# Attention: the turned FFN weight tile is split on POOL, and the inverse square roots of the q and k norms are one power operation each

## The reference

```python
q = (layernorm(x) @ Wq).reshape(B, Sq, H, D)
k = (ctx @ Wk).reshape(B, Skv, H, D)
v = (ctx @ Wv).reshape(B, Skv, H, D)
q = rmsnorm(q, gq)          # x * rsqrt(mean(x**2) + 1e-5) * g, over the 128 of a head
k = rmsnorm(k, gk)
attn = softmax(einsum('bqhd,bkhd->bhqk', q, k) * D ** -0.5)
x = x + einsum('bhqk,bkhd->bqhd', attn, v).reshape(B, Sq, H * D) @ Wo
```

## Time and profile before

| what | value |
|---|---|
| median of 3 runs | 2759.77 us (2758.46 to 2761.99) |
| profiled execution: its own time | 2749.03 us |
| its span | 2747.2 us |
| busy in the span | PE 2310.0 (84%), DVE 1898.2 (69%), POOL 1361.7 (50%), ACT 1235.3 (45%) |
| mean granted TensorE clock, of full speed | 0.911 |

### The profile page before, as it was taken

The page is one execution under the profiler, slowest core; times in us unless marked ns, Lnnn a source line. Parts: engine busy times, 40 slices in busy tenths (PEclk is TensorE's granted clock), DMA queues, the critical chain, the costliest instruction groups (busy, mean ns, idle before and its releaser), DMA issues. The chain is left out here.

```text
span 2747.2 us, 37910 instructions
## 1 busy us (share of the span) xinstructions
PE 2310.0 (84%) x10784; PEld 1774.8 (65%) x10785; DVE 1898.2 (69%) x3625; ACT 1235.3 (45%) x2129; POOL 1361.7 (50%) x1722
## 2 busy tenths in 40 slices
PE   3699999999999999998784898998998839459980
PEld 2687888878787878887533665665665426447770
DVE  6576777767677767776675989999999876412223
ACT  2353444544444444454483655655655412024440
POOL 0233333333243333332384888878988803478324
PEclk7799999999999999999886999999999958679995
DMA  7512232122322232220457555464665220565317
GB/s 276 206 62 101 85 109 86 62 90 85 109 85 76 76 109 85 85 77 28 142 202 237 176 180 184 173 197 151 205 195 158 86 89 16 201 201 175 130 54 256
DMA packets 136939, 363.84 MB, mean 132 GB/s; under 512 B 21280, under 2 KB 58912, under 8 KB 118560
## 3 DMA queue, kind: packets, MB, share of 16 engines
q1 hardware_dynamic: 123648, 328.36, 35.5%
q0 software_dynamic: 6320, 20.71, 2.4%
q10 hardware_dynamic: 6768, 12.32, 1.2%
HBM read 290.06 MB, written 71.30 MB: 132 GB/s over the span
## 5 line engine op out<-in xcount | busy, mean ns | idle before, releaser
L662 POOL TENSOR_SCALAR att_probs<-att_probs,att_recip 128x512 f32<-128x512 f32 x256 | 183.9, 722 | 402.5 <-DVE att_recip L743 398.1
L1837 POOL TENSOR_TENSOR mix_drive<-mix_du,mix_rows 128x512 f32<-128x512 f32 x256 | 326.5, 1282 | 61.4 <-DMA mix_rows<-bc_d 29.1
L585 ACT ACTIVATE att_probs<-att_s,att_bias,att_rq 128x512 f32<-128x512 f32 x256 | 199.9, 781 | 301.3 <-DVE att_bias L739 299.1
L1890 DVE TENSOR_TENSOR_SCAN mix_state<-mix_state,mix_drive 128x512 f32<-128x512 f32 x256 | 312.6, 1221 | 14.7 <-POOL mix_drive L1837 10.7
L1721 ACT ACTIVATE mix_state<-mix_delta,mix_a 128x512 f32<-128x512 f32 x256 | 176.7, 691 | 277.4 <-DVE mix_drive L1901 238.6
L1822 POOL TENSOR_TENSOR mix_y<-mix_y,mix_drive 128x512 f32<-128x512 f32 x180 | 230.6, 1281 | 79.0 <-DVE mix_drive L1901 79.0
L1630 PE MATMUL mix_down<-mix_wd,mix_hT 128*128 128x512 f32 x512 | 232.1, 596 | 8.7 <-DVE residual_x L1921 8.7
L738 DVE TENSOR_REDUCE att_nmax<-att_s 128x1 f32<-128x512 f32 x256 | 174.9, 683 | 64.7 <-PE att_s L101 64.7
L591 ACT CAST att_pT<-att_pt 128x512 fp32r<-128x512 f32 x256 | 143.4, 588 | 141.7 <-PE att_pt L442 137.6
L789 DVE TENSOR_TENSOR att_pT<-att_pt,att_pT 128x512 fp32r<-128x512 f32 x256 | 169.4, 682 | 44.6 <-ACT att_pT L591 44.2
L99 PE MATMUL att_w<-att_w_qkv,att_cx 128*128 128x256 f32 x512 | 161.9, 316 | 34.7 <-DVE att_w_qkv L725 26.7
(11 more groups left out here) (359 smaller groups left out, 6789.5 us busy)
## 6 DMA issues: line engine op xcount, KB each, us to landing
att_xn<-normT SPq DMA_DIRECT2D x32, 2048.0 KB, 9.2
mix_gu<-guT SPq DMA_DIRECT2D x64, 1024.0 KB, 8.3
mix_rows<-bc_d SPq DMA_DIRECT2D x128, 256.0 KB, 5.0
guT<-att_ffnT SPq DMA_DIRECT2D x32, 512.0 KB, 3.4
mix_wd<-wdT SPq DMA_DIRECT2D x16, 1024.0 KB, 7.8
slots<-exp_y ACTq DMA_DIRECT2D x47, 256.0 KB, 2.0
normT<-nrm_outT SPq DMA_DIRECT2D x4, 2048.0 KB, 9.1
exp_raw<-in_L_ffn_Wg SPq DMA_DIRECT2D x16, 512.0 KB, 5.8
```

Of the source, the lines that this page charges most:

```text
L585: act.activation(probs[:, n, :], ps_s[n % 2][:, :], ACT.Exp, bias=bias[:, n:n + 1], scale=rq[:, n:n + 1], accum_out=sums[:, n:n + 1]).then ...
L662: pool.tensor_scalar(probs[:, n, :], probs[:, n, :], recip[:, n:n + 1], 1.0, ALU.mult, ALU.mult).then_inc(s_pn, 1)
L1837: pool.tensor_tensor(drive[q % RING][:, :], du[i % DUS][:, :], rows[g % ROWS][:, 0, :], ALU.mult).then_inc(s_drive, 1)
L1890: dve.tensor_tensor_scan(h[:, :], h[:, :], drive[q % RING][:, :], 0.0, ALU.mult, ALU.add).then_inc(s_scan, 1)
```

## The change

Three things are changed, all in `stage_attention`.

1. The inverse roots. The three Newton steps on POOL and the two guess operations on DVE become one POOL operation, value to the power of a constant tile of -0.5, for k and for q.
2. The FFN tile. ACT, which wrote the hi of the turned tile to `fT`, now copies the whole float32 tile from PSUM back over `fraw` (`ffn_out`). POOL then makes both parts from it in SBUF (`split_ffn`), between `norm_p` 7 and the power of q. DVE's `ffn_lo` goes.
3. The waits. The FFN tile has semaphores of its own, so `turn_p(1, 1)`, which uses its PSUM bank, waits for ACT's copy and not for DVE. SP issues the load of `xn` as soon as the queries of j are done, ahead of its wait for the FFN tile; the load of the next FFN tile now waits for POOL's split, since `fraw` is used until then. At b = 0 the loads of weights stand ahead of that of `xn`.

```diff
@@ SP
+                sp.wait_ge(s_q, 2)
+                sp.dma_start(xn[:, :, :, :].bitcast(F32), xT[1]).then_inc(s_xn, 16)
                 def iteration(hp, b, last):
                     i = hp * B + b
-                    if not last:
-                        sp.wait_ge(s_q, 2 * i + 2)
-                        sp.dma_start(xn[:, :, :, :].bitcast(F32), xT[(b + 1) % B]).then_inc(s_xn, 16)
                     if b == 0 and not (isinstance(hp, int) and hp == PAIRS - 1):
...
+                    if not (isinstance(hp, int) and b >= B - 2):
+                        sp.wait_ge(s_q, 2 * i + 4)
+                        sp.dma_start(xn[:, :, :, :].bitcast(F32), xT[(b + 2) % B]).then_inc(s_xn, 16)
+                    sp.wait_ge(s_flo, i + 1)
                     if not last:
-                        sp.wait_ge(s_pt, TURNS * i + TB + 1)
                         load_ffn(hp + (b + 1) // B, (b + 1) % B)
-                    sp.wait_ge(s_ptlo, TURNS * i + TB + 1 + 2)
                     store_ffn(hp, b)
@@ PE, turn_p
-                    pe.wait_ge(s_ptlo, TURNS * i + n + 1)
+                    if h and k == 1:
+                        pe.wait_ge(s_fout, i + 1)
+                    elif h and k == 0:
+                        pe.wait_ge(s_ptlo, 8 * i + TB + 2)
+                    else:
+                        pe.wait_ge(s_ptlo, 8 * i + TB * h + k + 1)
@@ ACT
-                def ffn_hi(hp, i, b):
-                    act.wait_ge(s_pt, TURNS * i + TB + 1)
-                    act.wait_ge(s_fst, 16 * (i + 1))
-                    act.copy(fT[:, 0, :, :], ps_pt[(b + TB) % 2][:, :, :]).then_inc(s_fhi, 1)
+                def ffn_out(i, b):
+                    act.wait_ge(s_ft, i + 1)
+                    act.copy(fraw[:, :], ps_pt[(b + TB) % 2][:, :, :].rearrange("p k n -> p (k n)")).then_inc(s_fout, 1)
@@ POOL
-                def newton(own, out, value, guess, work):
...
+                def norm_k(j):
                     wait_apart(pool, s_kss, j + 1, s_pace)
-                    newton(own, rk[:, :], kss[:, :], kguess[:, :], work[:, :])
-                    pool.sem_inc(s_rk, 1)
+                    pool.tensor_tensor(rk[:, :], kss[:, :], power[:, :], ALU.pow).then_inc(s_rk, 1)
...
+                def split_ffn(i):
+                    parts = [fT[:, n, :, :].rearrange("p k n -> p (k n)") for n in range(2)]
+                    wait_apart(pool, s_fout, i + 1, s_pace)
+                    wait_apart(pool, s_fst, 16 * (i + 1), s_pace)
+                    pool.tensor_scalar(parts[0], fraw[:, :], 1.0, 1.0, ALU.mult, ALU.mult).then_inc(s_fhi, 1)
+                    wait_apart(pool, s_fhi, i + 1, s_pace)
+                    pool.tensor_tensor(parts[1], fraw[:, :], parts[0].bitcast(F32), ALU.subtract).then_inc(s_flo, 1)
...
                     if not last:
-                        norm_k(own, j)
+                        norm_k(j)
                     norm_p(i, 6)
                     norm_p(i, 7)
+                    split_ffn(i)
                     if not last:
-                        norm_q(own, j)
@@ DVE
-                    own.after(dve.tensor_scalar(kss[:, :], kss[:, :], 1.0 / D, RMS_EPS, ALU.mult, ALU.add))
-                    guess(own, kguess[:, :], kss[:, :]).then_inc(s_kss, 1)
+                    dve.tensor_scalar(kss[:, :], kss[:, :], 1.0 / D, RMS_EPS, ALU.mult, ALU.add).then_inc(s_kss, 1)
...
-                    ffn_lo(i, b)
                     o_lo(i, 0)
```

More of the change, by code:

```diff
@@ L260, in stage_attention @@
     RMS_EPS = 1e-5
-    NEWTON = 3
     scale = D ** -0.5
@@ L295, in stage_attention @@
         rq = m.sb("rq", [P, TB * HP])
-        kguess = m.sb("kguess", [P, TB * HP])
-        qguess = m.sb("qguess", [P, TB * HP])
-        work = m.sb("work", [P, TB * HP])
+        power = m.sb("power", [P, TB * HP])
         nmax = m.sb("nmax", [P, TB * HP])
@@ L331, in stage_attention @@
         s_pace = m.sem("pace")
-        s_fraw, s_fhi, s_fst = m.sem("ffn_raw_in"), m.sem("ffn_hi"), m.sem("ffn_stored")
+        s_fraw, s_ft, s_fout = m.sem("ffn_raw_in"), m.sem("ffn_turned"), m.sem("ffn_turned_out")
+        s_fhi, s_flo, s_fst = m.sem("ffn_hi"), m.sem("ffn_lo"), m.sem("ffn_stored")
         def pairs(eng, iteration):
@@ L636, in iteration @@
                         q_parts(j, 1)
-                    ffn_hi(hp, i, b)
+                    ffn_out(i, b)
                     o_hi(i, 0)
@@ L663, in norm_p @@
                                        ALU.mult).then_inc(s_pn, 1)
-                def newton(own, out, value, guess, work):
-                    cur = guess
-                    for _ in range(NEWTON):
-                        own.mark(pool.tensor_tensor(work, cur, cur, ALU.mult))
-                        own.wait_apart(s_pace)
-                        own.mark(pool.tensor_tensor(work, work, value, ALU.mult))
-                        own.wait_apart(s_pace)
-                        own.mark(pool.tensor_scalar(work, work, -0.5, 1.5, ALU.mult, ALU.add))
-                        own.wait_apart(s_pace)
-                        own.mark(pool.tensor_tensor(out, cur, work, ALU.mult))
-                        own.wait_apart(s_pace)
-                        cur = out
@@ L689, in _ @@
-                own = Steps(pool, s_pool)
-                square_k(0)
-                norm_k(own, 0)
-                norm_q(own, 0)
-                base = own.n
-                per_pair = B * base
-                def iteration(own, hp, b, last):
+                    pool.tensor_tensor(rq[:, :], qss[:, :], power[:, :], ALU.pow).then_inc(s_rq, 1)
+                def split_ffn(i):
[5 more added lines that the diff above has]
+                    pool.tensor_tensor(parts[1], fraw[:, :], parts[0].bitcast(F32), ALU.subtract).then_inc(s_flo, 1)
@@ L697, in iteration @@
+                pool.memset(power[:, :], -0.5).then_inc(s_power, 1)
+                square_k(0)
+                pool.wait_ge(s_power, 1)
+                norm_k(0)
+                norm_q(0)
+                def iteration(hp, b, last):
                     i = hp * B + b
@@ L705, in iteration @@
                     if not last:
-                        norm_k(own, j)
+                        norm_k(j)
                     norm_p(i, 6)
                     norm_p(i, 7)
+                    split_ffn(i)
                     if not last:
-                        norm_q(own, j)
-                with pool.Fori(0, PAIRS - 1) as hp:
-                    own = Steps(pool, s_pool, hp * per_pair + base)
-                    for b in range(B):
-                        iteration(own, hp, b, False)
-                own = Steps(pool, s_pool, (PAIRS - 1) * per_pair + base)
-                for b in range(B):
-                    iteration(own, PAIRS - 1, b, b == B - 1)
+                        norm_q(j)
+                pairs(pool, iteration)
             @block.vector
@@ L743, in row_recip @@
                     dve.reciprocal(recip[:, n:n + 1], sums[:, n:n + 1]).then_inc(s_rec, 1)
-                def guess(own, out, value):
-                    I32 = mybir.dt.int32
-                    own.after(dve.tensor_scalar(out.bitcast(I32), value.bitcast(I32), 1, None, ALU.logical_shift_right))
-                    return dve.tensor_scalar(out.bitcast(I32), out.bitcast(I32), -1.0, float(0x5F3759DF), ALU.mult, ALU.add)
                 def sum_k(own, j):
@@ L824, in _ @@
                 kt_lo(0, 1)
-                sum_q(own, 0)
+                sum_q(0)
                 v_lo(0, 0)
@@ L832, in _ @@
                 base = own.n
-                per_pair = B * (8 + 3 + 1) + 3
+                per_pair = B * (8 + 1) + 3
                 def iteration(own, hp, b, last):
@@ L873, in iteration @@
                     if not last:
-                        sum_q(own, j)
+                        sum_q(j)
                     pt_lo(i, b, 1, 3)
```

31 lines of the change are left out of this document (10 added, 21 removed).

## The result

The changed kernel takes 2714.74 us (median of 4 runs, 2706.9 to 2728.31); the kernel before, run beside it, takes 2759.11 us (4 runs, 2754.12 to 2761.99). The ratio is 0.985, with a 95% interval of 0.9822 to 0.9878. That is 44 us saved, where 30 were forecast. 2714.74 lies inside the range, but only just: the lower end was 2714 for the forecast's own case and 2712 for 8 in 10. The profiled execution took 2715.96 us, its span is 2714.2 us.

A forecast was written before the change was run, and what follows sets the result against it. PE's work was taken to bound the attention stage. Waits 10 and 2, start 4 and clock 14 us sum to 30, from 2759.8 to 2730 us; own range 2714 to 2750, 8 in 10 within 2712 to 2770.

The forecast's parts named there:

- DVE without `ffn_lo`: Lo of k and what follows on DVE move earlier, ending PE's wait before q's sums: 10 us, bounds 0 and 12.
- k's root: In the loop, a power under 4.4 us ends PE's 7 waits for the normed k: 2 us.
- The guesses ahead of the lo of p (0, 0): Two guesses leaving DVE save 0.4 us there, but PE has no gap: gain 0.
- The start: At the stage's start PE waits 5.50 us for the first normed k; the power saves 4 us (0.5 to 4.9).
- The clock: Fewer falls of PE's clock behind q's sums: 14 us, bounds 0 and 26.
- q's root: q's inverse root on POOL is already 3 us early for its first use on DVE: gain 0.
- the load of xn: SP issues it 3.4 us or more sooner, but its reader is half an iteration away: 0.
- POOL's split: POOL splits the FFN tile in idle time, from 655.5 to about 657.8: cost 0.
- rival C: POOL's subtraction blocks scale_k's eighth piece if the copy ends before it starts; k 1.3 us late, 2786 us; chance 0.10.
- A: PE's clock stays as before, only waits and start count: 16 us, 2744; chance 0.22. Other end, all falls go: 2718.
- B: Nothing gained: the 0.3 us return as another PE wait and the power eats the start's gain; 2755 to 2764; chance 0.09.
- D: POOL's power is slow: each us above 4.4 costs 31 us; at 8 us about 2870; chance 0.09.

The follow-up runs named there:

- e4_guess_kept: Changed kernel with DVE's two guess operations for k's root put back, result unread; 2716.39 us in one run.
- e3_dve_refilled: Changed kernel with an unused 0.67 us reduction on DVE where the FFN tile's subtraction stood, plus a wait ahead of the loop; 2728.03 us, ratio 0.9898.
- e1_split_only: Changed kernel with Newton and its guesses kept, so only the FFN tile's split on POOL and the waits change; 2741.17 us, ratio to before 0.9946.
- e9_sums_apart: Changed kernel with PE's column sums of q in two groups, the first head's between two halves of a product of v; 2691.14 us, ratio 0.979.
- e5_pad8: Changed kernel with eight more semaphore increments, read by nobody, ahead of DVE's loop; 2714.04 us, ratio 0.9857.
- e10_pe_pad20: Changed kernel with 20 more semaphore increments, read by nobody, ahead of PE's loop; 2711.51 us, ratio 0.9863.
- e6_xn_behind: Changed kernel with the load of xn put back behind SP's wait for the FFN tile's split; 2716.52 us in one run.
- e8_power_k4: Changed kernel with three more powers of the k sums, unread, on POOL ahead of the used one; 2837.22 us in one run.
- e7_scale_late: Changed kernel with DVE's lo of q's second head moved ahead of scale_k, so scale_k starts later; 2776.29 us in one run.

## Why the prediction was right

The sign, the place and the bound were right: PE bounds the stage, and it gained where it stood still and where its clock fell. The sum came out by luck in part: terms that were too large (10 us for `ffn_lo`, 14 for the clock) met others that were too small or missing. I lay the 40.6 us that the two profiled executions differ by in the stage beside the terms.

**DVE without `ffn_lo`, 10 us.** The wait went, but it was laid to the wrong edit: the power alone takes it away, with `ffn_lo` still on DVE, and both together are worth no more. The argument on ACT was right, the lo of k can't start ahead of ACT's hi of k. But DVE was only 0.23 us behind that, and the power, which lets `scale_k` start sooner and makes it shorter, was enough to win it. PE's gain at that place is 0.18 us per step, 31 x 0.18 = 6 us, and not the 0.31 of its wait.

**k's root, 2 us.** Too small. It counted only the 7 waits that the profile lists, but PE's transposes of k moved up against the product before by 0.26 us on the mean of the 23 ordinary steps (0.17 to 0.46 by kind of step), mostly under what the list shows. That is 6 us in them alone. Here `scale_k` starts sooner and loses a `norm_p` from beside it. I took its length as given.

**The guesses ahead of the lo of p (0, 0), 0.** Wrong in size: 0.12 to 0.15 us per step, at the third turn of p (`e4_guess_kept`). On the mean of the 23 ordinary steps the three places make 0.13 + 0.26 + 0.18 = 0.57 of the 0.69 us that a step saves. The rest is in the third kind of step, where PE's wait for the lo of o ahead of the projections was 0.60 us in the one step without a slow stretch and is 0.25 now; over three kinds that is 0.1. Together 12 us were forecast for these terms, 20 were measured over 29 steps.

**The start, 4 us.** 4.2, when PE's earlier first product is taken off. The power takes 1.65 us where I took 1, so PE's wait fell to 2.18 us and not to 1.5, by 3.3 us, near the 4.7 + 0.4 - 1.65 = 3.45 of k's chain. The rest is the clock. Before, `turn_k` and the sums ran wholly at half clock, 1.97 and 3.41 us; now they take 1.25 and 2.46.

**The clock, 14 us.** 8 slow stretches fewer, 10.4 us, within the bounds of 0 and 26; with the 8 to 13 of the kernels that have after's gap it is 9 to 16. That it takes more than the wait was right. `e3_dve_refilled`, where the gap alone goes back from 0.42 to 0.57, has 18 again and points to the gap as a cause. In `e1_split_only` and `e9_sums_apart` other things moved with it, a wait ahead of `turn_k` and half of the sums.

**The branches, not named.** The 6 steps with a branch gave 1.67 us each and not 0.69, 6 us more. One pause of DVE moved from ahead of the second reciprocal to ahead of a later row maximum, behind the bias that the first exponential waits for, and is half as long. The exponential that waits for this later one (1.1 us in one such step) no longer holds PE. This is an effect of the length of DVE's program and not of the change's idea. That the pause hangs on the code's length ahead of and in the loop is shown by `e5_pad8`, `e10_pe_pad20` and `e4_guess_kept`; why it does is open.

**What costs nothing.** q's root, the load of xn (`e6_xn_behind`) and POOL's split: as forecast. But the split's 0 hung on a margin of 0.3 to 0.4 us (rival C).

**Rivals.** A's lower half (the clock stays) and B fell by the result. C and D were tried. C's blocked piece costs 1.1 us for 1.3; its condition, the copy's end against the eighth piece's start, was misplaced by one piece, for behind a copy that held up the seventh (split only) the eighth still got in ahead of the subtraction. D's threshold stands within 0.2 us; the one point above it cost 1.8 and not 1 per us.

## What to carry to other kernels

When two edits of one change free the same late engine, run each alone: here the one-operation root gave all of it, and moving the split to POOL bought nothing more and brought a two-input POOL operation within 0.3 to 0.4 us of `scale_k`. Then ask what the freed engine waits for next: here it was ACT, and past that point no work taken off DVE counted. Don't price a wait of 0.3 us by its length alone: next to a piece of one-column products it went with how often TensorE's clock fell, and moving half of that piece into the wait was worth 20 us, about 10 for the wait filled and the rest for the clock. In a loop whose bound engine pauses at the branch with nothing that it waits for, look at the packets of the instruction queues and shift the code on all engines that pause, for one alone gained under 1 us per branch here.

## What the runs showed of the hardware

- POOL's power on 128x8 values takes 1.65 us (median of q's and k's), against 4.7 us for Newton's twelve operations in the earlier trace rows; one of q's took 2.10, in the row shown above.
- A one-tensor operation of DVE in SBUF, 0.27 us, that starts once POOL's has begun ends within 0.1 us of it: 0.64 beside a `norm_p`, 0.67 beside the copy (0.62), 1.34 beside an operation with two tensors (1.26). A piece that starts before the subtraction isn't held (the eighth of split only). The eight pieces took 1.66, 2.00, 2.39, 2.77, 3.12 and 4.01 us, by what lay beside them.
- Across the kernels the clock fell less often behind the sums the less PE stood still ahead of them (the table above), and in the kernels with 8 to 13 falls the time of one kernel varied by up to 21 us between runs (after); with the piece in two, by 2 to 7 us. With a longer wait elsewhere (3.3 us, `e8_power_k4`) 20 falls stand behind that; one of 2.0 us (`e7_scale_late`) made only 4. What divides these two cases is open.
- PE and DVE pause twice after the loop's branch, mostly 1.1 to 2.6 us each, where no wait is shown. 8 increments ahead of DVE's loop, or 20 ahead of PE's, took both pauses of that engine away, and 31 and 54 packets of its instruction queue. The runs show that pauses and packets go together, not why.
